# Masked and first units' values one unit later, value weights behind x, x stored block by block

## The chip, the cores and the metric

The kernel runs on the 8 cores of one Trainium2 chip. Every core does the whole transformer layer for one of the eight sequences and talks to no other core, so the program is the same everywhere. The metric is the device time in microseconds of the slowest core; lower is better.

## The reference

```python
x = _layernorm(x + attn(x))        # x: (8, 4096, 1024), one sequence per core
x = _layernorm(x + ffn(x))
# attn: qkv = x @ Wqkv.T + b; 16 heads of 64; causal softmax(q k.T / 8) v; @ Wproj.T + b
# ffn:  gelu(x @ w1 + b1) @ w2 + b2, hidden width 4096
```

The products run in bfloat16 with float32 sums in PSUM.

## The kernel before

**Stages.** A core first computes attention for 8 pairs of heads (p = 0 to 7), each over 8 blocks of 512 queries (g = 0 to 7), and then goes through 16 blocks of 256 tokens with the output projection, the first norm and the feed-forward layer. x lies transposed in the tile `xT` during attention: 128 partitions, and per partition 8 feature chunks (fc) of 4096 tokens each, so that token block g of chunk fc begins at column 4096 fc + 512 g. The input in DRAM (`xb`) is laid out by block.

**Units.** Attention is a list of 1088 units (p, g, j). A unit is one key tile j of 128 keys against the 512 queries of block g for both heads of pair p: scores (L593, TensorE, into one of two pairs of PSUM banks, by the unit's parity), exp (L610, ScalarE, into one of 7 buffers `pbuf`), for the tiles on the diagonal a mask (L621, VectorE), and the values (L665, TensorE: 8 matmuls of 65 columns for each 128 queries, into banks 6 and 7). A block has 4g + 3 units; the last three are on the diagonal (j = 4g, 4g + 1, 4g + 2; the second also carries tile 4g + 3). The first eight blocks of pairs 0 and 1 alternate, then the pairs follow one after another. After a block's last values VectorE divides by the row sums (`divide`, L688 and L690), which also frees banks 6 and 7 for the next block's first unit; some units later `turn_block` transposes the result (L704), copies it (L708) and stores it in DRAM.

**What sets the order.** The instruction order of each engine is written out by the loop at L944. Iteration i puts any waiting halves of values, scores of unit i + 1, exp of unit i, again halves of values, perhaps one `turn_block`, and then fill: `run_fill` takes steps from the queue `fill` by a credit that spreads them up to the unit that needs them. The fill steps are the projections of q and k (`qk_steps` L284, `qk_pairs` L452/L453), their row norms for the exp's bound (L312, L512), and the values' projection (`v_steps` L375, `v_pairs`). Each step has a `need` and a `free`, the first unit at which it may be put. `waiting` holds units whose values are not yet queued: the oldest is queued at iteration i once i minus its number reaches `hold`, which is 3 for a block's first unit (j = 0) and 2 otherwise. `run_halves` puts a unit's values in two halves of 64 key rows, the second only after something else was put between.

**Start.** `pool.dma` issues on GpSimd's queue, in this order: q and k weights of pair 0 (two pieces `wqk0_0`, `wqk0_4`), x of block 0 in four pieces of two chunks each, and the value weights of the first group in two pieces (`wv0_0`, `wv0_4`), interleaved as w, x, wv, x, w, x, wv, x; then the weights of pair 1, x of blocks 1 to 7, and more weights. Each piece is 256 KB as it lies on chip. SyncE's queue brings the mask (`tri`, behind x's first piece), biases and the identity. Meanwhile TensorE does 40 matmuls on constants (`warm`, L239). `first_block` then does, chunk by chunk, the q and k projection (`go`, L404: two matmuls of 512 columns) and the values' projection (`go_v`, L412: four matmuls of 256 columns) of block 0, then VectorE adds the bias (L423), TensorE does the scores of unit 0 and the two norm sums (L431), VectorE the maxima (L435) and the bound (L329, L338), and last the values' evacuation (L439). ScalarE's first instruction is the exp of unit 0, ahead of which the table is loaded.

**Other loads.** `wp` is loaded into `wpT` at the head of block (3, 1), behind pair 2's last values, because pair 2's q and k lie there; the first eight pieces of w2 are issued at the head of (7, 1), behind pair 6's last values and the w1 pieces. At the head of (7, 0) GpSimd adds the projection's bias to two blocks of x (`add_bias`, L774).

Of the kernel before, what the change touches and what calls it, by code (L numbers as in the profile page):

```python
# [10 lines left out]
AF = mybir.ActivationFunctionType  # L11
# [75 lines left out]
def build_nc():  # L87
# [115 lines left out]
    xTv = xT.rearrange("p (f g c) -> p f g c", f=8, g=NG)  # L203
    ld_bqk = sp.dma(slot("bqk"), bqk, bqk_d)
    first_x, ld_qk0, ld_v0 = [], [], []
    wqk0 = wqk[0].rearrange("p (i c) -> p i c", i=2)
    wqk0_d = wqk_d[0].rearrange("p (i c) -> p i c", i=2)
    for f in range(0, 8, 2):
        if f % 4 == 0:
            ld_qk0.append(pool.dma(slot(f"wqk0_{f}"), wqk0[:, :, 128 * f : 128 * f + 512],  # L210
                                   wqk0_d[:, :, 128 * f : 128 * f + 512]))
        first_x.append(pool.dma(
            slot(f"x0_{f}"), xTv[:, f : f + 2, 0, :],
            xb_d[0][:, QB * f : QB * f + 2 * QB].rearrange("p (f c) -> p f c", f=2)))
        if f % 4 == 0:
            ld_v0.append(pool.dma(slot(f"wv0_{f}"), wv[0][:, 256 * f : 256 * f + 1024],
                                  wv_d[0][:, 256 * f : 256 * f + 1024]))
    ld_qk[0], ld_v[0] = ld_qk0[1], ld_v0[1]
    ld_qk[1] = pool.dma(slot("wqk1"), wqk[1], wqk_d[1])
    for g in range(1, NG):  # L220
        ld_x[g] = pool.dma(slot(f"x{g}"), xTv[:, :, g, :],
                           xb_d[g].rearrange("p (f c) -> p f c", f=8))
# [13 lines left out]
    def warm():  # L236
        a = None
        for _ in range(40):
            r = t.matmul(bank(6), ones, sq[0], start=True, stop=True)  # L239
            a = a or r  # L240
        return a, r
    warm_done = pe.put(warm, t_warm, t_ones)
# [28 lines left out]
    def qk_steps(p, qi, g):  # L271

        st = {}
        w = wqk[QK_AT[p]]

        def step(fc):
            def go():
                if fc == 0:
                    st["b"] = gbank(True)
                b = st["b"]  # L280
                last = fc == 7
                gb_open[b] = not last
                tok = pe.put(
                    lambda: t.matmul(  # L284
                        bank(4 + b),
                        w[:, 1024 * qi + 128 * fc : 1024 * qi + 128 * fc + 128],
                        xT[:, S * fc + QB * g : S * fc + QB * g + QB],
                        start=fc == 0, stop=last),
                    *((gb_free[b], ld_qk[p], ld_x[g]) if fc == 0 else ()), mark=last)
                if last:  # L290
                    dst = (q2 if qi == 0 else k2)[p][:, QB * g : QB * g + QB]
                    ev = dve.put(
                        lambda: v.tensor_scalar(
                            dst, bank(4 + b), bqk[:, 8 * qi + p : 8 * qi + p + 1], None, ALU.add),
                        tok, ld_bqk, q2_done.get(QK_FROM.get(p)))
                    gb_free[b] = ev
                    t_qk[p, qi, g] = ev
                    wqk_done[p] = tok
            return go
        return [(1.0, step(fc)) for fc in range(8)]  # L300
# [58 lines left out]

    def v_steps(vp, a):  # L360
# [4 lines left out]
        def step(h):  # L365
            def go():
# [5 lines left out]
                for fc in (2 * h, 2 * h + 1):  # L372
# [4 lines left out]
                            xT[:, S * fc + 128 * a : S * fc + 128 * a + 128],  # L377
# [17 lines left out]
    def first_block():  # L395
# [4 lines left out]
        def go(fc):  # L400
            r = a = None
            for qi in range(2):
                o = 1024 * qi + 128 * fc
                r = t.matmul(bank(4 + qi), wqk[0][:, o : o + 128], xT[:, S * fc : S * fc + QB],  # L404
                             start=fc == 0, stop=fc == 7)
                a = a or r
            return a, r

        def go_v(fc):
            r = a = None  # L410
            for n in range(4):
                r = t.matmul(bank(6 + n // 2)[:, 256 * (n % 2) : 256 * (n % 2) + 256],  # L412
                             xT[:, S * fc + 128 * n : S * fc + 128 * n + 128],
                             wv[0][:, 256 * fc : 256 * fc + 256],
                             start=fc == 0 and n % 2 == 0, stop=fc == 7, skip_group_check=True)
                a = a or r
            return a, r
        for fc in range(8):
            tok = pe.put(lambda fc=fc: go(fc), first_x[fc // 2], ld_qk0[fc // 4], mark=fc == 7)
            tok_v = pe.put(lambda fc=fc: go_v(fc), ld_v0[fc // 4], mark=fc == 7)  # L420
# [15 lines left out]
        bound(0, 0)  # L436
        for a in range(4):
# [30 lines left out]
    def qk_pairs(p, g):  # L468
# [4 lines left out]
        def step(n):  # L473
            def go():
# [6 lines left out]
                xs = slice(S * fc + QB * g, S * fc + QB * g + QB)  # L481
# [41 lines left out]
    def v_pairs(vp, a):  # L523
# [4 lines left out]
        def step(n):  # L528
            def go():
# [4 lines left out]
                c0, c1 = (S * fc + 128 * (a + b0), S * fc + 128 * (a + b1))  # L534
# [370 lines left out]
    for p, g in blocks:  # L905
        if p > 1 or g > 3:
            need = start_of[p, g] if p < NPAIR - 1 else start_of[p, 0]
            later.append((need, qk_pairs(p, g) + norm_pair(p, g), start_of[p - 1, 0] + 3 if p > 2 else 0))
            if p % 2 == 0:
                vs = [x for a in range(4 * g, 4 * g + 4, 2) for x in v_pairs(p // 2, a)]  # L910
                later.append((need + 4 * g, vs, start_of[p - 2, 0] + 3 if p > 2 else 0))
# [31 lines left out]

    for i, (p, g, j) in enumerate(units):  # L944
        if j == 0:
            if (p, g) == (3, 1):
# [8 lines left out]
            if p == NPAIR - 1 and g == 1:  # L955
                load_w2(0, 8, q2_done[NPAIR - 2])
# [17 lines left out]
        hold = 3 if units[waiting[0]][2] == 0 and i + 1 < NU else 2  # L974
        while waiting and i - waiting[0] >= hold:
            queue_values(waiting.popleft())
            hold = 2
# [190 lines left out]
```

How the kernel before makes its waits and increments, by code:

```python
    def run(self):  # L54
        seen = {}
        for emit, after, inc in self.items:
            waits = {}
            for tok in after:
                if tok is None:
                    continue
                sem, val = tok
                if seen.get(sem, 0) >= val:
                    continue
                waits[sem] = max(waits.get(sem, 0), val)
            for sem, val in waits.items():
                seen[sem] = val
            todo = list(waits.items())
            held = todo.pop() if (todo and self.fuse) else None
            for sem, val in todo:
                self.eng.wait_ge(sem, val)
            done = emit()
            first, last = done if isinstance(done, tuple) else (done, done)
            if held is not None:
                first.wait_op(held[0], held[1], "sem-ge")
            if inc is not None:
                last.then_inc(inc[0], inc[1])
```

## Time and profile before

| what | us |
|---|---|
| median of 3 runs | 2211.36 |
| the three runs | 2211.36, 2312.66, 2210.08 |
| the profiled execution | 2209.44 |
| its span on the slowest core (core 1) | 2207.9 |
| spans of the 8 cores | 2200.8 to 2207.9 |
| granted TensorE clock, mean of core 1 | 0.986 |
| TensorE matmuls busy (PE) | 2059.6 |
| ScalarE busy (ACT) | 1328.7 |
| VectorE busy (DVE) | 743.2 |

The profile is of one execution on its slowest core, in microseconds from its first instruction. PE is TensorE's matmuls, PEld its weight loads, DVE VectorE, ACT ScalarE, POOL GpSimd, SPq SyncE's queue. A row of a group of instructions gives line, engine, operation, output<-input by tile (many tiles share the name `work`), shapes and count, busy time and the mean of one in ns, and then the engine's idle time before them with what ended it. A busy time of several matmuls run together ends with the last one's pipeline, so it is not the spacing times their number. The clock is 1.00 for 2.4 GHz and 0.50 for 1.2 GHz.

### The profile page before, as it was taken

The numbers are of one execution on the slowest core, as the hardware profiler recorded it, in microseconds if no ns is written. First come the engines' busy times: TensorE is split into PE (matmuls) and PEld (weight loads), VectorE is DVE, ScalarE is ACT, GpSimd is POOL, SyncE is SP. The second block draws the span as 40 slices with busy tenths as digits, with TensorE's granted clock in tenths as the row PEclk, the third lists the DMA queues.
The fourth block names the chain that finished last, engine by engine and source line by source line (L and its number), as shares of the span: only waits on it lengthen the run. The fifth ranks groups of instructions, "written<-read, shape, count | busy, mean of one in ns | idle before, by whom it ended". The sixth has DMA issues, their size and how long they took to land.

```text
span 2207.9 us, 65222 instructions; the slowest of 8 cores (2200.8 to 2207.9 us)
## 1 busy us (share of the span) xinstructions
PE 2059.6 (93%) x30380; PEld 1299.5 (59%) x30380; DVE 743.2 (34%) x1925; ACT 1328.7 (60%) x1602; POOL 219.2 (10%) x182
## 2 busy tenths in 40 slices
PE   7999998989999999997788999999999999999997
PEld 3455565555565556654445666666666666666665
DVE  3543334344343443435121322333223223332321
ACT  1799999999999999998995222222222222222222
POOL 2000000000000000001011221222111112221100
PEclk8999999999999999999899999999999999999999
DMA  9500100021000000002954201111110011111000
GB/s 144 81 12 8 36 8 12 19 34 35 8 13 19 8 24 8 12 10 66 169 88 89 51 27 48 49 49 49 48 48 20 30 48 48 48 48 49 20 20 20
DMA packets 53184, 89.73 MB, mean 41 GB/s; under 512 B 3248, under 2 KB 36656, under 8 KB 51888
## 3 DMA queue, kind: packets, MB, share of 16 engines
q0 software_dynamic: 17184, 33.56, 10.0%
q1 hardware_dynamic: 35728, 52.00, 7.1%
q8 instruction: 237, 3.88, 0.7%
q14 instruction: 35, 0.29, 0.0%
HBM read 93.94 MB, written 25.17 MB: 54 GB/s over the span
## 4 chain that ended last, share of the span: by engine, by line
PE 61%; ACT 29%; DVE 7%; DMA 1%; issue 1%; POOL 0%; POOLq 0%; SPq 0%; DVEq 0%; ACTq 0%
ACT work L610 29%; PE ps L1010 20%; PE ps L1028 19%; PE ps L815 5%; PE ps L452 5%; PE ps L665 4%; PE ps L593 4%; DVE qkv L493 2%; DVE work L621 1%; PE ps L284 1%; PE ps L512 1%; DVE work L690 1%; DMA xT<-xb 1%; DVE stat L517 1%; PE ps L858 1%
## 5 line engine op out<-in xcount | busy, mean ns | idle before, releaser
L610 ACT ACTIVATE work<-ps,cb 128x1024 bf16<-128x1024 f32 (+1 forms) x1088 | 1083.8, 1123 | 66.6 <-PE ps L593 61.6
L1018 ACT ACTIVATE work<-ps,b_s 128x256 bf16<-128x256 f32 x512 | 242.3, 473 | 764.1 <-PE ps L1010 764.1
L665 PEld LDWEIGHTS ps<-qkv,work 64*128 64x128 bf16 x16896 | 434.6, 95 | 292.7 <-PE ps L665 82.7
L665 PE MATMUL ps<-qkv,work 64*128 64x65 bf16 x16896 | 569.8, 193 | 17.9 <-DVE work L690 11.6
L1010 PE MATMUL ps<-work,xT 128*128 128x256 bf16 x4096 | 532.2, 273 | 0.4 <-issue 0.4
L1028 PE MATMUL ps<-qkv,work 128*128 128x512 bf16 x1984 | 509.0, 379 | 0.0
L1010 PEld LDWEIGHTS ps<-work,xT 128*128 128x128 bf16 x4096 | 401.3, 98 | 156.2 <-issue 0.5
L593 PE MATMUL ps<-qkv 64*128 64x512 bf16 x2016 | 366.4, 369 | 65.4 <-ACT work L610 57.8
L1028 PEld LDWEIGHTS ps<-qkv,work 128*128 128x128 bf16 x1984 | 192.9, 98 | 164.1 <-ACT work L1018 0.2
L452 PE MATMUL ps<-xT,work 64*128 64x512 bf16 x896 | 258.3, 377 | 2.9 <-DVE stat L517 1.8
L453 PE MATMUL ps<-xT,work 64*128 64x512 bf16 x896 | 258.4, 377 | 0.0
L593 PEld LDWEIGHTS ps<-qkv 64*128 64x128 bf16 x2016 | 94.5, 94 | 114.5 <-ACT work L610 93.4
L621 DVE TENSOR_TENSOR work<-work,tri_s 128x128 bf16<-128x128 bf16 x512 | 92.2, 238 | 199.5 <-ACT work L610 199.3
L815 PE MATMUL ps<-wpT,work 128*128 128x512 bf16 x512 | 146.3, 380 | 0.8 <-DMA work<-attn_s 0.6
L1054 DVE TENSOR_TENSOR work<-ps,work 128x512 f32<-128x512 f32 x64 | 39.8, 684 | 309.0 <-PE ps L1028 309.0
L452 PE MATMUL ps<-work,xT 64*128 64x256 bf16 x896 | 134.0, 269 | 3.4 <-DVE stat L517 1.8
L453 PE MATMUL ps<-work,xT 64*128 64x256 bf16 x896 | 134.0, 269 | 0.0
L493 DVE TENSOR_SCALAR qkv<-ps,bqk_s 128x512 bf16<-128x512 f32 x96 | 67.5, 745 | 156.5 <-PE ps L453 156.5
L774 POOL TENSOR_TENSOR work<-work,bvb 128x1024 f32<-128x1024 f32 x32 | 75.2, 2351 | 422.8 <-DMA work<-x 420.3
L788 POOL TENSOR_TENSOR lnst<-lnst,cexp 128x1 f32<-128x1 f32 x64 | 35.1, 548 | 629.5 <-DVE lnst L787 627.5
L790 DVE SCALAR_TENSOR_TENSOR lnst<-lnst 128x1 f32<-128x1 f32 x64 | 10.2, 160 | 234.2 <-POOL lnst L788 234.2
L546 DVE TENSOR_TENSOR qkv<-ps,bvb 128x256 bf16<-128x256 f32 x112 | 42.4, 421 | 136.0 <-PE ps L453 136.0
(74 smaller groups left out, 1262.2 us busy)
## 6 DMA issues: line engine op xcount, KB each, us to landing
work<-x SPq DMA_DIRECT2D x16, 1024.0 KB, 6.3
out<-work SPq DMA_DIRECT2D x15, 1024.0 KB, 4.1
attn_s<-work SPq DMA_DIRECT2D x64, 128.0 KB, 2.0
xT<-w POOLq DMA_DIRECT2D x8, 1024.0 KB, 14.6
work<-attn_s SPq DMA_DIRECT2D x16, 512.0 KB, 7.7
qkv<-w POOLq DMA_DIRECT2D x16, 512.0 KB, 8.3
xT<-xb POOLq DMA_DIRECT2D x7, 1024.0 KB, 45.4
work<-wqk POOLq DMA_DIRECT2D x7, 512.0 KB, 6.1
```

Of the source, the lines that this page charges most:

```text
L452: x = t.matmul(out0, lhs0, rhs0, start=start, stop=stop, skip_group_check=True)
L453: y = t.matmul(out1, lhs1, rhs1, start=start, stop=stop, skip_group_check=True)
L493: lambda qi=qi, dst=dst: v.tensor_scalar(dst, bank(4 + qi), bqk[:, 8 * qi + p : 8 * qi + p + 1], None, ALU.add),
L593: b = t.matmul(PS[:, o : o + 512 - q0], k2[p][64 * h : 64 * h + 64, 128 * jt : 128 * jt + 128], q2[p][64 * h : 64 * h + 64, QB * g + q0 : ...
L610: lambda: sc.activation(pb, ps, AF.Exp, bias=cb[:, 8 * p + g : 8 * p + g + 1], scale=0.125),
L621: b = v.tensor_tensor(q, q, tri_s, ALU.mult)
L665: r = t.matmul(bank(6 + h)[:, 65 * c : 65 * c + 65], pbuf[i % NP][rows, pc : pc + 128], w[rows, o : o + 65], start=first and j == 0 and c ...
L774: lambda c=c: gp.tensor_tensor(xbuf[n][:, 1024 * c : 1024 * c + 1024], xbuf[n][:, 1024 * c : 1024 * c + 1024], bpb, ALU.add),
L815: lambda: t.matmul(out_bank, atb[b % 2][:, 256 * k + 128 * c : 256 * k + 128 * c + 128], wpT[:, 1024 * k + 512 * oh : 1024 * k + 512 * oh ...
L1010: r = t.matmul(bank(4 + ui % 2)[:, 0:TB], w1[:, FF * f + 128 * hc : FF * f + 128 * hc + 128], x2T[b % 2][:, TB * f : TB * f + TB], start=f ...
L1018: lambda: sc.activation(hbuf[ui % 4], bank(4 + ui % 2)[:, 0:TB], AF.Gelu, bias=b1[:, hc : hc + 1]),
L1028: r = t.matmul(bank(2 * c + oh), hbuf[ui % 4][:, 128 * c : 128 * c + 128], w2[hc][:, 512 * oh : 512 * oh + 512], start=hc == 0, stop=hc == 31)
```

## The change

The change has five parts. (1) The value weights `wv0` come in one transfer behind the four pieces of x, and `go_v` is now put once, behind the two norm sums and ahead of the scores of unit 1, instead of chunk by chunk between the q and k projections. (2) `xT` is laid out by block: block g begins at column 4096 g, with its 8 chunks of 512 inside; a transfer's run in a partition becomes 2 KB (pieces) or 8 KB (blocks) where it was 1 KB. (3) `warm` is 26 matmuls ahead, and 3, 3, 3 and 4 more behind each pair of chunks. (4) ScalarE does a small exp at the start. (5) A unit's values are queued 4 units after it for j = 0, 3 for the diagonal's units, and 2 otherwise; `free` of later pairs' fill goes from + 3 to + 6, `wp` from (3, 1) to (3, 2), and w2 from (7, 1) to (7, 2).

```diff
@@ start: the transfers
-        first_x.append(pool.dma(
-            slot(f"x0_{f}"), xTv[:, f : f + 2, 0, :],
-            xb_d[0][:, QB * f : QB * f + 2 * QB].rearrange("p (f c) -> p f c", f=2)))
-        if f % 4 == 0:
-            ld_v0.append(pool.dma(slot(f"wv0_{f}"), wv[0][:, 256 * f : 256 * f + 1024],
-                                  wv_d[0][:, 256 * f : 256 * f + 1024]))
-    ld_qk[0], ld_v[0] = ld_qk0[1], ld_v0[1]
+        first_x.append(pool.dma(slot(f"x0_{f}"), xT[:, QB * f : QB * f + 2 * QB],
+                                xb_d[0][:, QB * f : QB * f + 2 * QB]))
+    ld_qk[0] = ld_qk0[1]
+    ld_v[0] = pool.dma(slot("wv0"), wv[0], wv_d[0])
     ld_qk[1] = pool.dma(slot("wqk1"), wqk[1], wqk_d[1])
     for g in range(1, NG):
-        ld_x[g] = pool.dma(slot(f"x{g}"), xTv[:, :, g, :],
-                           xb_d[g].rearrange("p (f c) -> p f c", f=8))
+        ld_x[g] = pool.dma(slot(f"x{g}"), xT[:, 8 * QB * g : 8 * QB * g + 8 * QB], xb_d[g])
@@ warm-up and table
-    def warm():
+    def warm(n):
         a = None
-        for _ in range(40):
+        for _ in range(n):
             r = t.matmul(bank(6), ones, sq[0], start=True, stop=True)
             a = a or r
         return a, r
-    warm_done = pe.put(warm, t_warm, t_ones)
+    pe.put(lambda: warm(26), t_warm, t_ones)
+    act.put(lambda: sc.activation(lnst[:, 0:1], cexp[:, 0:1], AF.Exp), t_cexp)
@@ qk_steps (and alike in v_steps, first_block, qk_pairs, v_pairs)
-                        xT[:, S * fc + QB * g : S * fc + QB * g + QB],
+                        xT[:, 8 * QB * g + QB * fc : 8 * QB * g + QB * fc + QB],
+    def x_col(a, fc):
+        return 8 * QB * (a // 4) + QB * fc + 128 * (a % 4)
@@ first_block
-        def go_v(fc):
+        def go_v():
             r = a = None
             for n in range(4):
-                r = t.matmul(bank(6 + n // 2)[:, 256 * (n % 2) : 256 * (n % 2) + 256],
-...
+                for fc in range(8):
+                    r = t.matmul(bank(6 + n // 2)[:, 256 * (n % 2) : 256 * (n % 2) + 256],
+                                 xT[:, x_col(n, fc) : x_col(n, fc) + 128],
+                                 wv[0][:, 256 * fc : 256 * fc + 256],
+                                 start=fc == 0 and n % 2 == 0, stop=fc == 7, skip_group_check=True)
+                    a = a or r
             return a, r
         for fc in range(8):
             tok = pe.put(lambda fc=fc: go(fc), first_x[fc // 2], ld_qk0[fc // 4], mark=fc == 7)
-            tok_v = pe.put(lambda fc=fc: go_v(fc), ld_v0[fc // 4], mark=fc == 7)
+            if fc % 2 == 1:
+                warm_done = pe.put(lambda: warm(3 if fc < 7 else 4), t_warm, t_ones)
...
         bound(0, 0)
+        tok_v = pe.put(go_v, ld_v[0])
@@ fill of later pairs
-            later.append((need, qk_pairs(p, g) + norm_pair(p, g), start_of[p - 1, 0] + 3 if p > 2 else 0))
+            later.append((need, qk_pairs(p, g) + norm_pair(p, g), start_of[p - 1, 0] + 6 if p > 2 else 0))
...
-                later.append((need + 4 * g, vs, start_of[p - 2, 0] + 3 if p > 2 else 0))
+                later.append((need + 4 * g, vs, start_of[p - 2, 0] + 6 if p > 2 else 0))
@@ main loop
+    def behind(p, g, j):
+        return 4 if j == 0 else 3 if j >= 4 * g else 2
...
-            if (p, g) == (3, 1):
+            if (p, g) == (3, 2):
...
-            if p == NPAIR - 1 and g == 1:
+            if p == NPAIR - 1 and g == 2:
                 load_w2(0, 8, q2_done[NPAIR - 2])
...
-        hold = 3 if units[waiting[0]][2] == 0 and i + 1 < NU else 2
-        while waiting and i - waiting[0] >= hold:
+        while waiting and (i + 1 == NU or i - waiting[0] >= behind(*units[waiting[0]])):
             queue_values(waiting.popleft())
-            hold = 2
```

## Rows read from the trace of the kernel before

**Rows 1.** the page: engines, then exp and values (busy us, mean ns | idle).

```profile
PE 2059.6 (93%) x30380; PEld 1299.5 (59%) x30380; DVE 743.2 (34%) x1925; ACT 1328.7 (60%) x1602; POOL 219.2 (10%) x182
...
L610 ACT ACTIVATE work<-ps,cb 128x1024 bf16<-128x1024 f32 (+1 forms) x1088 | 1083.8, 1123 | 66.6 <-PE ps L593 61.6
...
L665 PE MATMUL ps<-qkv,work 64*128 64x65 bf16 x16896 | 569.8, 193 | 17.9 <-DVE work L690 11.6
```

**Rows 2.** by stretch: length, busy us of PE, PEld, DVE, ACT, POOL; clock, DMA, GB/s.

```profile
30.00:119.00 89.00, 78.22 (x1112) 37.93 (x1108) 48.75 (x138) 56.22 (x54) 0.00 (x0) 0.97 0.65 98
119.00:1034.00 915.00, 838.24 (x19741) 520.70 (x19738) 367.32 (x1099) 891.30 (x897) 4.60 (x8) 1.00 0.08 19
1034.00:1060.00 26.00, 15.67 (x338) 10.01 (x336) 15.49 (x33) 18.82 (x21) 11.15 (x7) 0.74 0.61 123
1060.00:1182.00 122.00, 94.74 (x2216) 58.39 (x2216) 26.38 (x83) 118.76 (x121) 14.15 (x17) 0.93 0.60 101
1182.00:2207.90 1025.90, 1010.33 (x6894) 662.56 (x6886) 280.55 (x560) 243.59 (x513) 175.95 (x128) 0.99 0.14 44
```

**Rows 3.** the timeline's DMA issues: start us, length, engine, line, operation, transfer.

```profile
10.15 0.33 SPq L50 DMA_DIRECT2D tri_s<-tri  x1
...
25.58 0.33 SPq L50 DMA_DIRECT2D bvb<-bv  x1
```

**Rows 4.** the timeline of TensorE, VectorE, ScalarE, 3 to 32 us; idle before in brackets.

```profile
3.05 10.88 PE L239 MATMUL ps<-work,ones 128*128 128x512 bf16 x40 [3.05 <-DVE work L234]
...
16.80 0.60 PE L412 MATMUL ps<-work,xT 128*128 128x256 bf16 x4
...
18.88 0.59 PE L404 MATMUL ps<-xT,work 128*128 128x512 bf16 x2 [1.47 <-DMA xT<-xb]
...
22.73 1.03 PE L404 MATMUL ps<-xT,work 128*128 128x512 bf16 x2 [0.77 <-DMA xT<-xb]
...
25.26 1.06 PE L412 MATMUL ps<-work,xT 128*128 128x256 bf16 x4
...
25.59 1.41 DVE L423 TENSOR_SCALAR qkv<-ps,bqk_s 128x512 bf16<-128x512 f32 x2 [22.60 <-PE ps L404]
...
27.59 1.03 PE L431 MATMUL ps<-work,ones 128*128 128x512 bf16 x2
...
29.59 0.61 PE L593 MATMUL ps<-qkv 64*128 64x384 bf16 x4 [0.96 <-DVE stat L435]
...
30.00 1.28 ACT L610 ACT_TABLE_LOAD   x1 [30.00 <-DVE cb L338]
...
30.13 5.38 PE L284 MATMUL ps<-xT,work 128*128 128x512 bf16 x14
...
31.29 2.12 ACT L610 ACTIVATE work<-ps,cb 128x1024 bf16<-128x1024 f32 x2
```

**Rows 5.** busy times before and after the clock's first fall, columns as in the second group.

```profile
16.80:20.97 4.17, 2.12 (x14) 1.07 (x13) 0.00 (x0) 0.00 (x0) 0.00 (x0) 1.00 1.09 178
20.97:34.60 13.63, 11.16 (x36) 4.10 (x35) 6.17 (x16) 3.40 (x3) 0.00 (x0) 0.50 1.00 147
```

**Rows 6.** waits of ScalarE and TensorE, 119 to 1034 us; total, times, longest.

```profile
ACT work L610 <- PE ps L593: 23.6, 50, 2.1
...
PE ps L665 <- DVE work L690: 8.2, 21, 0.8
```

**Rows 7.** groups of instructions, 1034 to 1046 us.

```profile
L621 DVE TENSOR_TENSOR work<-work,tri_s 128x128 bf16<-128x128 bf16 x16 | 10.3, 719 | 3.3 <-ACT work L610 3.3
L774 POOL TENSOR_TENSOR work<-work,bvb 128x1024 f32<-128x1024 f32 x4 | 9.6, 2390 | 264.9 <-DMA work<-x 264.5
...
L665 PE MATMUL ps<-qkv,work 64*128 64x65 bf16 x82 | 3.1, 196 | 4.3 <-DVE work L621 4.3
```

**Rows 8.** the tile xT, 0 to 130 us: durations ns minimum/median/maximum, and DMA landing.

```profile
L284 PE MATMUL ps<-xT,work x112: 376/379/634, 30.1 to 115.3; 128*128 128x512 bf16 x112
...
L50 POOL DMA_DIRECT2D xT<-xb x11: 713/873/889, 2.5 to 12.8; - x11
...
DMA to landing us min/median/max: 7.6/34.4/63.8
```

More of the change, by code:

```diff
@@ L202, in build_nc @@
     ld_v = {}
-    xTv = xT.rearrange("p (f g c) -> p f g c", f=8, g=NG)
     ld_bqk = sp.dma(slot("bqk"), bqk, bqk_d)
-    first_x, ld_qk0, ld_v0 = [], [], []
+    first_x, ld_qk0 = [], []
     wqk0 = wqk[0].rearrange("p (i c) -> p i c", i=2)
@@ L376, in go @@
                             bank(4 + b)[:, 0:256],
-                            xT[:, S * fc + 128 * a : S * fc + 128 * a + 128],
+                            xT[:, x_col(a, fc) : x_col(a, fc) + 128],
                             w[:, 256 * fc : 256 * fc + 256],
@@ L403, in go @@
                 o = 1024 * qi + 128 * fc
-                r = t.matmul(bank(4 + qi), wqk[0][:, o : o + 128], xT[:, S * fc : S * fc + QB],
+                r = t.matmul(bank(4 + qi), wqk[0][:, o : o + 128], xT[:, QB * fc : QB * fc + QB],
                              start=fc == 0, stop=fc == 7)
@@ L407, in go @@
             return a, r
-        def go_v(fc):
+        def go_v():
             r = a = None
             for n in range(4):
-                r = t.matmul(bank(6 + n // 2)[:, 256 * (n % 2) : 256 * (n % 2) + 256],
[L413 to L416, printed above, removed]
+                for fc in range(8):
[4 more added lines that the diff above has]
+                    a = a or r
             return a, r
@@ L480, in go @@
                 o1 = 1024 * qi1 + 128 * fc
-                xs = slice(S * fc + QB * g, S * fc + QB * g + QB)
+                xs = slice(8 * QB * g + QB * fc, 8 * QB * g + QB * fc + QB)
                 tok = two_tiles(
@@ L533, in go @@
                 b0, b1 = (1, 0) if turned else (0, 1)
-                c0, c1 = (S * fc + 128 * (a + b0), S * fc + 128 * (a + b1))
+                c0, c1 = x_col(a + b0, fc), x_col(a + b1, fc)
                 ws = slice(256 * fc, 256 * fc + 256)
```

## The prediction

> **What bounds the kernel now.** I read the page's busy times first, then busy times by stretch, the timeline of the start, the waits, and the groups around the one large stall. TensorE is busy 2059.6 us and ScalarE 1328.7, which says little by itself [rows 1]. The stretches say more [rows 2]. From 1182 us on TensorE is busy 1010.3 of 1025.9 us: the feed-forward stage is TensorE's, and no part of the change touches it. From 119 to 1034 us ScalarE is busy 891.3 of 915 us: there the exps set the pace, and the most that any reordering can give is the 23.7 us that ScalarE stands idle. From 30 to 119 us ScalarE is busy only 56.2 of 89 us while TensorE is busy 78.2: the projections of the first blocks must be caught up with, so a microsecond won ahead of this stretch is passed on to its end. Before 30 us nothing is computed that ScalarE could use: it waits until 30.00 and loads its table until 31.29 [rows 4]. Over the whole span the exp's engine was idle 66.6 us ahead of its exps, 61.6 of it for scores [rows 1]. That is 3.0% of the span and the ceiling of the attention parts.
>
> **The start.** x's first piece had landed by 10.15 us [rows 3], its last at 22.73 [rows 4]. Between them lie six pieces of 256 KB, 12.6 us, 2.1 us each; the last two took 22.73 - 18.88 = 3.85 us, 1.9 each. Two of the eight, the value weights, go behind x, so the last piece lands 3.9 to 4.2 us earlier, at about 18.7 us. GpSimd issues in the same queue, one transfer fewer; its issue of a piece takes 0.7 to 0.9 us [rows 8] and ends long before the landing, so it stays covered.
>
> At 22.73 us the clock had already fallen to 0.50 (it fell at 20.97 and came back at 34.60 [rows 5]), and eight value matmuls stood between and behind the last four of q and k, so VectorE's bias began only at 25.59, 2.86 us behind the landing [rows 4]. Two 512-column matmuls take 0.59 us at the full clock and 1.03 at half [rows 4], where one alone takes 0.38 and 0.63 [rows 8]: a spacing of 0.21 and about 0.42. The four that are left cost 0.9 or 1.7 us. The bias then begins at 19.6 us at the full clock; at half it begins at 20.4, or at 21.3 if the two matmul pairs and three warm-ups ahead are late as well.
>
> From the bias to the bound were 30.00 - 25.59 = 4.4 us, with the two norm sums at half clock (1.03 us; 0.59 at full). The table's 1.28 us [rows 4] now lies at the start, where ScalarE has nothing else. The first exp moves from 31.29 to 23.6 (full) or 25.7 us (half).
>
> That is not yet the gain, since the values' projection no longer sits in the shadow of the transfers: 32 matmuls of 256 columns now stand in TensorE's queue ahead of the scores of unit 1. Four take 0.60 us at full and 1.06 at half clock [rows 4], a spacing of 0.11 and 0.21: 3.5 or 6.9 us for all. They begin behind the norm sums, 3.0 us (2.6 at full) behind the bias, and not before their weights, which end the same eight pieces as before and so land near 22.8 us. At the full clock: 22.8 + 3.5 = 26.3, scores of unit 1 by 26.9, then the first fill, 14 matmuls that took 5.38 us from 30.13 [rows 4] and take 13 x 0.21 + 0.38 = 3.1 at full. They end at 30.0 where they ended at 35.5: 5.5 us won. At half: values from 24.3; before, the clock returned at 34.60 after 5 us of steady work from 29.59 [rows 4, 5]; if it does the like, at 29.3, the values end near 30.2 and the fill at 33.9: 1.6 us won. Which of the two? Before, 2.12 busy us of 4.17 were followed by the fall [rows 5]. Now, from the end of 26 warm-ups (14 fewer of 0.21 us, so about 10.9 us) to 18.7 us there are three rounds of four matmuls and three warm-ups, 7 x 0.21 = 1.5 us each, 4.5 us of 7.8, 58% against 51%. That is too near to promise the full clock; the fall may come somewhat later. I take **3.0 us**, with 1.6 and 5.5 as ends.
>
> The layout of x changes no matmul: each still reads 512 contiguous columns of a partition. For the transfers the rows leave room for a gain: pair 1's weights, 512 KB in 4 KB runs, landed 2.85 us behind x's last piece (25.58 - 22.73 [rows 3, 4]), 180 KB per us; the seven blocks of x behind them, 7168 KB in 1 KB runs, landed 63.8 us after an issue at 12.8 [rows 8], so at 76.6, 141 KB per us. At the better rate x's four pieces would land 1.5 us earlier. But the pieces of the start moved at 256 / 1.9 = 135 KB per us whatever their runs, so I take 0, and keep -1.5 as an end. The Trainium skill, DMA: Bandwidth & Descriptors, section Specifications, has line rate from 512 bytes on, by which 1 KB runs already had it and this part gives nothing; the 141 against 180 speaks for a difference, and measurement would decide. No wait of the start is on blocks 1 to 7, so their faster landing is worth nothing.
>
> On the table the Trainium skill, ScalarE: Activation LUTs, section What ACT_TABLE_LOAD costs, has 1.28 us and about 1.38 of drain for a switch. The trace agrees with the first (1.28) and shows no second: the exp begins at 31.29, where the load ends [rows 4]. By the page the start would give 1.4 us more.
>
> **The stall at 1034 us.** GpSimd's four adds (9.6 us) make 16 masks take 10.3 us, 0.65 each, and TensorE waits 4.3 us for masks in values that stand ahead of scores [rows 7]. From 1034 to 1060 us ScalarE is idle 7.2 us, and the clock is at 0.74 [rows 2]. The adds and the masks stay. One unit more lies between a mask and its values, so one more exp can run first, at most an exp's 1.0 us (891.3 / 897 [rows 2]) and the clock's share of it. I take **1.5 us**, between 0 and 3.
>
> **The other turns.** From 119 to 1034 us TensorE's waits on this side are for the divide (8.2 us, 21 times) and not for masks, which the view does not list at all [rows 6]. The change does not help the divide: the last unit's values move by one (2 to 3) and the next first unit's by one (3 to 4), so the divide has the same two units. What moves is where the matmuls lie. When the first unit's values are queued, two other units' come at once instead of one. I take **0.5 us** of gain; the ends are a third of the 23.6 us of waits [rows 6], -8, and +8, the divide's waits doubled.
>
> **Moved loads.** `wp` waits for pair 2's last values, now a unit (1.0 us) later, and is read some 500 us later; on GpSimd's queue nothing is put between. The w2 pieces stand behind the w1 pieces in the same queue, so their place in the program costs nothing. If w2's cover were gone the feed-forward stage would show it as a wait of at most the moved seven units, 7 us. `free` + 6 binds only where fill is that far ahead; where it binds, 3 units of about 1 us do without fill and catch up by at most 3 steps each, five times: 0 to 5 us, taken as 0.
>
> The sum: 2209.4 (the profiled execution; its span is 2207.9) - 3.0 - 1.5 - 0.5 = 2204.4, rounded to **2204 us**. The profiled execution lies 2.0 us under the median of the runs, 2211.36, so against that the gain is 7 us, 0.3%.
>
> **Rivals.** (a) Start's gain lost: the clock falls early, stays at half through the values and does not return with them, so that the second scores are as late as before and only the other terms stay: 2207 to 2210. For it speaks the 51% row; against it that the values and fill are now one steady run. (b) Slower: the values bunch. At some 60 turns two held units come behind a first one, and TensorE has little room to catch up: it is busy 838 of 915 us, 0.09 us free per exp [rows 2]. A unit's values are 569.8 / 1088 = 0.52 us [rows 1]. If all of that comes ahead of scores and isn't absorbed, 60 x 0.52 = 31 us are lost: 2204 + 31 = 2235. It decides as soon as the extra unit exceeds what the one pair of scores computed ahead can cover, about an exp less its scores, 0.6 us; 0.52 is under it, and the present hold of 3 already bunches one unit and costs at most the 23.6 us of all waits. So rather a third of it, 2215, if it comes. (c) The turns gain for real: half of the ScalarE waits of 23.6 go, and the start keeps its 5.5: 2204 - 12 - 2.5 = 2190. For it: 50 waits of half a us are of a size with one unit's shift. (d) Part of the change doesn't do what it says: ScalarE's table could be loaded at the first exp anyway, 1.3 us less gain; 2206, inside the forecast.
>
> **How the numbers follow.** The forecast, 2199 to 2208, has 0.5; (a) 0.17; (b) 0.16; (c) 0.14; anything outside 0.03. The range 2190 to 2217 holds the forecast, (a), most of (c) and the lower half of (b). Faster by over 2% would need 44 us, two thirds of all idle time ahead of exps: 0.01. Slower by over 2%, more than (b) in full: 0.02. Within 2%, about what a measurement of this kernel can tell from no change: 0.97.
>
> **What would show it.** The bias on q and k near 20 us instead of 25.59; a table load before 5 us and the first exp near 24 to 26; the clock's first fall later than 20.97 or missing; `L284`'s first fourteen ending between 30 and 34 instead of 35.5; ScalarE's waits from 119 to 1034 near 23 us; its idle time from 1034 to 1060 nearer 6 than 7.2. Waits above 32 us there would show (b), under 14 (c). The stage from 1182 on must keep its 1026 us; if it doesn't, the prediction is wrong in a part I costed at nothing.

## The result and the profile after

The change made the kernel slower: the ratio to the kernel before is 1.0063, 95% interval 1.0044 to 1.0082, about 14 us on 2210. The medians of 13 runs each are 2223.72 and 2210.89 us; the profiled execution took 2220.25 us, its span was 2218.7 (2207.9 before). The predicted 2204 was wrong in sign, and the median lies above the whole predicted range, 2190 to 2217. Some executions of either kernel are disturbed, up to 2490 us, and are left out of all ratios.

The start, from the timeline of the changed kernel (start us, length, engine, line, operation, tiles, count, idle before), answers to [rows 3, 4]. Its lines are numbered anew: L280 was L284, L404 stays, L413 is the values' projection, L613 the exp (L610), L668 the values (L665), L693 the divide (L690), L707 the transposes (L704), L624 the mask (L621). L515 is the pairs' norm sums (L512), L501 the VectorE step ahead of them (L498).

```profile
1.05 1.28 ACT L238 ACT_TABLE_LOAD   x1 [1.05 <-PEq L88]
...
16.04 1.02 PE L404 MATMUL ps<-xT,work 128*128 128x512 bf16 x4 [1.03 <-DMA xT<-xb]
...
17.41 0.32 SPq L50 DMA_DIRECT2D idb_s<-idb  x1
17.77 1.03 PE L404 MATMUL ps<-xT,work 128*128 128x512 bf16 x4
...
18.91 1.41 DVE L425 TENSOR_SCALAR qkv<-ps,bqk_s 128x512 bf16<-128x512 f32 x2 [15.93 <-PE ps L404]
...
21.27 3.66 PE L413 MATMUL ps<-work,xT 128*128 128x256 bf16 x32
...
22.90 1.11 ACT L613 ACTIVATE work<-ps,cb 128x1024 bf16<-128x1024 f32 x1 [20.18 <-DVE cb L334]
...
25.18 3.19 PE L280 MATMUL ps<-xT,work 128*128 128x512 bf16 x14
...
41.42 0.69 ACT L613 ACTIVATE work<-ps,cb 128x512 bf16<-128x512 f32 x1 [7.02 <-PE ps L596]
```

x's last piece has landed by 17.41 us, where the identity behind it is issued, instead of at 22.73. The bias begins at 18.91 instead of 25.59. The first fill's fourteen matmuls end at 28.37 instead of 35.51 [rows 4], 7.1 us ahead. That sets core 0 of the changed kernel against core 1 of the kernel before, whose start was the latest of its eight. Core by core the same matmuls end 1.9 to 6.3 us earlier, 4.3 on the mean (28.4 against 32.7), so the start is ahead by less than the 7.1 suggests. By stretches the changed kernel reads (columns as in [rows 2]):

```profile
0.00:30.00 30.00, 24.63 (x117) 11.22 (x117) 8.71 (x23) 4.25 (x5) 9.77 (x21) 1.00 0.95 141
30.00:119.00 89.00, 76.61 (x1205) 38.54 (x1207) 46.42 (x137) 57.31 (x57) 0.00 (x0) 1.00 0.54 94
119.00:1034.00 915.00, 828.56 (x19414) 514.26 (x19414) 363.69 (x1083) 877.29 (x882) 4.63 (x8) 0.99 0.08 17
1034.00:1192.00 158.00, 117.72 (x2737) 73.78 (x2733) 45.16 (x118) 146.43 (x149) 25.34 (x24) 0.89 0.61 109
1192.00:2218.70 1026.70, 1011.20 (x6920) 663.22 (x6919) 281.37 (x565) 245.08 (x515) 176.12 (x128) 0.99 0.14 43
```

The feed-forward stage has its time, 1026.7 us for 1025.9. From 119 to 1034 us ScalarE is idle 37.7 us where it was 23.7 (means of the eight cores: 35.8 and 22.5), and did 882 exps where it did 897. So the place is the turns. The prediction's sign for its rival (b), ScalarE's waits there above 32 us, has come (36.1), but it can't tell bunched values from another cause at the same turns. The waits of that stretch in the changed kernel (engine and line, what it waited for: total us, times, longest) answer to [rows 6]:

```profile
ACT work L613 <- PE ps L596: 36.1, 64, 1.7
PE ps L596 <- ACT work L613: 40.7, 118, 0.6
PE ps L515 <- DVE work L501: 15.5, 25, 1.3
PE ps L707 <- DVE work L693: 14.6, 12, 1.9
PE ps L515 <- DVE work L711: 2.3, 5, 0.8
PE ps L707 <- DVE qkv L496: 2.0, 7, 0.5
PE ps L668 <- DVE work L693: 1.9, 5, 0.4
```

The fourth row is new. TensorE waited 14.6 us in 12 waits for the divide ahead of the transposes; before, no such row was there. The values' own wait for the divide fell from 8.2 to 1.9 us. One turn in the changed kernel's timeline shows the damage:

```profile
632.61 0.69 DVE L693 TENSOR_TENSOR work<-ps,rden 128x512 bf16<-128x512 f32 x1
633.36 0.61 PE L707 MATMUL ps<-idb_s,work 128*128 128x128 bf16 x4 [1.81 <-DVE work L693]
633.90 0.40 PE L668 MATMUL ps<-qkv,work 64*128 64x65 bf16 x8
634.07 0.42 DVE L711 COPY work<-ps 128x512 bf16<-128x512 bf16 x1 [0.77 <-PE ps L707]
634.11 0.62 PE L596 MATMUL ps<-qkv 64*128 64x512 bf16 x2
...
634.77 1.11 ACT L613 ACTIVATE work<-ps,cb 128x1024 bf16<-128x1024 f32 x1 [1.66 <-PE ps L596]
635.10 1.03 PE L515 MATMUL ps<-work,ones 128*128 128x512 bf16 x2
```

TensorE stands 1.81 us at the transposes, the scores behind them come late, ScalarE is idle 1.66 us, and then two 512-column matmuls take 1.03 us: the granted clock fell to 0.50 (1.2 GHz) near 633.2 us, at the end of the wait.

### The profile page after: what moved, and what is told of

Read it like the earlier page. It is cut to its first block, busy times and chain, and to the rows that moved or that the text cites. A ratio compares the mean times of both kernels' runs of the same rounds, so it can differ in the third digit from the quotient of the medians.

```text
span 2218.7 us, 65228 instructions; the slowest of 8 cores (2214.8 to 2218.7 us)
## 1 busy us (share of the span) xinstructions
PE 2058.7 (93%) x30382; PEld 1301.0 (59%) x30382; DVE 745.4 (34%) x1925; ACT 1330.4 (60%) x1603; POOL 215.9 (10%) x181
## 4 chain that ended last, share of the span: by engine, by line
PE 62%; ACT 28%; DVE 8%; issue 1%; DMA 1%; POOL 0%; POOLq 0%; ACTq 0%; DVEq 0%
ACT work L613 28%; PE ps L1016 20%; PE ps L1034 19%; PE ps L455 5%; PE ps L818 5%; PE ps L668 5%; PE ps L596 4%; DVE qkv L496 2%; PE ps L515 1%; DVE work L624 1%; DVE work L693 1%; PE ps L280 1%; PE ps L707 1%; DVE work L501 1%; PE ps L1043 1%
## 5 line engine op out<-in xcount | busy, mean ns | idle before, releaser
L613 ACT ACTIVATE work<-ps,cb 128x1024 bf16<-128x1024 f32 (+1 forms) x1088 | 1084.7, 1114 | 105.5 <-PE ps L596 80.7
L668 PEld LDWEIGHTS ps<-qkv,work 64*128 64x128 bf16 x16896 | 430.7, 96 | 267.7 <-PE ps L668 81.5
L668 PE MATMUL ps<-qkv,work 64*128 64x65 bf16 x16896 | 558.3, 193 | 6.4 <-DVE work L624 4.2
L624 DVE TENSOR_TENSOR work<-work,tri_s 128x128 bf16<-128x128 bf16 x512 | 92.7, 239 | 192.7 <-ACT work L613 191.8
```

The source lines that it names most:

```text
L613: lambda: sc.activation(pb, ps, AF.Exp, bias=cb[:, 8 * p + g : 8 * p + g + 1], scale=0.125),
L624: b = v.tensor_tensor(q, q, tri_s, ALU.mult)
L668: r = t.matmul(bank(6 + h)[:, 65 * c : 65 * c + 65], pbuf[i % NP][rows, pc : pc + 128], w[rows, o : o + 65], start=first and j == 0 and c ...
```

## The experiments

The theory after the result, D: the last unit's values come one unit later, but `turn_block` is still put 5 units after the block's last unit, so the transposes now stand one unit behind the divide in TensorE's queue instead of two, with scores behind them. Rivals: B, the held units' values bunch behind the first one; F, the fill held back to + 6; L, the new layout; S, the start's gain does not last.

**The start alone.**

```diff
-        while waiting and (i + 1 == NU or i - waiting[0] >= behind(*units[waiting[0]])):
+        hold = 3 if units[waiting[0]][2] == 0 and i + 1 < NU else 2
+        while waiting and i - waiting[0] >= hold:
             queue_values(waiting.popleft())
+            hold = 2
# free + 3, wp at (3, 1), w2 at (7, 1), as before
```

> The changed kernel with the order of values, free and the places of the loads as before, so parts 1 to 4 alone. In the profile of the changed kernel the fourteen matmuls of the first fill ended 7.1 us earlier (28.37 against 35.51 us), and at 54 us the exps were still 7.0 us ahead. Theory T (the start gives its 7 us, the order of the values takes it back and more): 2203 to 2205 us against 2211 before. Rival S (the start's gain is lost again somewhere in the projections' stretch whatever the order): 2208 to 2212. Rival L (the new layout of x slows the matmuls or transfers later): 2215 and more.

Ratio 0.998, interval 0.9962 to 0.9997; median 2204.03. L falls. The start gains about 4.4 us by the ratio and 7.5 by the medians; the ratio's interval reaches from 8 us to under 1, so the time alone does not rule S out. The traces do better. On the mean of the eight cores the exp that the rows above have at 41.42 us stands at 41.9 us, where it was 46.4 before; GpSimd's first add at the head of pair 7 stands at 1027.0, where it was 1031.2; ScalarE's table load at the end of attention stands at 1179.7, where it was 1182.6. So 4.5 us are won at the start, 4.1 last through the projections' stretch to the head of pair 7, against S, and 2.9 are left behind attention. T's direction holds; its 7 us were too much.

**The order alone**, the kernel before with part 5.

```diff
-        hold = 3 if units[waiting[0]][2] == 0 and i + 1 < NU else 2
-        while waiting and i - waiting[0] >= hold:
+        while waiting and (i + 1 == NU or i - waiting[0] >= behind(*units[waiting[0]])):
# free + 6, wp at (3, 2), w2 at (7, 2)
```

> The kernel before with part 5 alone: values of masked units 3 and of first units 4 behind, free + 6, wp and w2 a block later. Theory T: 12.8 us measured loss of the whole plus 7 us of the start, so 2228 to 2232 us. Rival L (layout): about 2211. If the two parts do not add (the order costs only because the start is ahead), 2215 to 2222.

Ratio 1.0093, interval 1.0078 to 1.0108, some 20 us; the profiled execution took 2229.49. The transposes' wait is there again, with the start as it was:

```profile
PE ps L704 <- DVE work L690: 14.5, 11, 1.9
```

The time is the one that T asked for, 2228 to 2232. The parts add within their intervals: -0.2% and +0.93% against +0.63%.

**The transposes one unit later.**

```diff
-        while turns and i - turns[0][0] >= 5 and not (gb_open[0] and gb_open[1]) and i >= ready[0]:
+        while turns and i - turns[0][0] >= 6 and not (gb_open[0] and gb_open[1]) and i >= ready[0]:
```

> The changed kernel with the transposes of a finished block put no earlier than 6 units after its last unit, where it was 5. The last values now end a unit later, so at 5 the transposes stand directly behind the divide in TensorE's queue, ahead of scores. Theory D (the loss at the turns is TensorE's wait of the transposes for the divide, 14.6 us in 12 waits from 119 to 1034 us, 0 before): the wait goes to under 3 us, time 2206 to 2212. Rival B (the values of three units come at once behind the first unit): the transposes' wait may go but the time stays within 3 us of 2222. Rival F (free + 6 and the burst of fill behind it): no change either, 2220 to 2224.

Ratio 0.9994, interval 0.998 to 1.0009. One number takes back 0.69% of the kernel's time, most of the 0.83% that lie between the changed kernel and the start alone, and of the transposes' 14.6 us of waiting 2.0 are left. ScalarE's waits stay above those of the start alone, 28.0 us against 20.3:

```profile
ACT work L613 <- PE ps L596: 28.0, 58, 1.3
...
PE ps L668 <- DVE work L693: 5.2, 14, 0.5
...
PE ps L707 <- DVE work L693: 2.0, 2, 1.8
```

**The transposes one unit sooner, values where they were.** The converse, on the start alone: only the distance is shortened.

```diff
-        while turns and i - turns[0][0] >= 5 and not (gb_open[0] and gb_open[1]) and i >= ready[0]:
+        while turns and i - turns[0][0] >= 4 and not (gb_open[0] and gb_open[1]) and i >= ready[0]:
```

> The start alone, values where they were before, with the transposes put from 4 units after a block's last unit, where it was 5. Only their distance to the divide is as short as in the changed kernel; nothing is bunched and no values are later. Theory D (that distance alone makes the loss): TensorE waits 12 to 18 us in about a dozen waits for the divide ahead of the transposes from 119 to 1034 us, and the time goes from 2204 to 2214 to 2220 us. Rival B (the later values' bunching makes it): 2203 to 2207.

Ratio 1.0032, interval 1.0004 to 1.0059; median 2216.35. No unit's values are later here and no more of them are queued at once, yet the kernel is 0.5% slower than the start alone, with the same kind of wait:

```profile
PE ps L707 <- DVE work L693: 12.1, 9, 2.8
```

So the distance by itself makes a loss, 0.5% here, of the 0.83% that the whole order costs on top of the start. D holds in both directions.

**Only first units later.**

```diff
-        return 4 if j == 0 else 3 if j >= 4 * g else 2
+        return 4 if j == 0 else 2
```

> The changed kernel with only first units one later (4), masked units at 2 as before. The last unit's values and the divide are then as early as before, but at the first unit's turn three units' values are queued at once, as in the changed kernel. Theory D: the transposes do not wait, and the time is that of the start's part, 2203 to 2208. Rival B (bunching): about as slow as the changed kernel, 2218 to 2224.

Ratio 0.9995, interval 0.9985 to 1.0004; median 2210.38. The transposes wait for the divide once, 0.8 us, the values once, 0.4 us. It queues three units at once, as the changed kernel does, and lies 13 (medians) to 15 us (ratios) below it; but it lies above the start alone, by 0.15%, with intervals that overlap, and its median is 2 us over D's range. A small price of bunching three is not ruled out.

**Only masked units later.**

```diff
-        return 4 if j == 0 else 3 if j >= 4 * g else 2
+        return 3 if j == 0 or j >= 4 * g else 2
```

> The changed kernel with masked units 3 behind and first units at 3 as before, transposes still at 5. The last unit's values and so the divide are a unit later, the next first unit's values are not. Theory D: the transposes wait as in the changed kernel (12 to 16 us), and the first unit's values now wait for the divide too, so it is as slow or slower, 2220 to 2232 us. Rival B (bunching of three units is what costs): without a bunch it is back at 2204 to 2210.

Ratio 1.0182, interval 1.0168 to 1.0197, and a median of 2250.39, slower than was expected even of D. The mechanism is D's, the place another: the next block's first values now stand one unit behind the divide and take the wait ahead of the transposes. The rows are of core 4, whose span is 2245.0 us:

```profile
PE ps L668 <- DVE work L693: 44.8, 47, 2.7
PE ps L596 <- ACT work L613: 29.1, 87, 0.5
```

44.8 us in 47 waits at the turns, against 8.2 in 21 [rows 6]. B asked for a return to the time before, since no three units are queued at once; the kernel is 40 us slower than that.

**First units five behind.** The changed kernel with transposes at 6, `free` + 3, and

```diff
-        return 4 if j == 0 else 3 if j >= 4 * g else 2
+        return 5 if j == 0 else 3 if j >= 4 * g else 2
```

> The changed kernel with transposes at 6 and free + 3, masked units 3 behind and first units 5 instead of 4, so that three units lie between the last values of a block and the first of the next, and four units' values are then queued at once. Theory D (only the distance to the divide counts): the waits of values for the divide, 5.2 us with 4, go to under 1 us and the time is 2203 to 2206. Rival B (bunching has a price that grows with the units queued at once): 2210 to 2222.

Ratio 1.0041, interval 1.0028 to 1.0054. Here the theory's number missed and B's came (median 2219.04): the values' wait for the divide went to 1.0 us as expected, yet the kernel is 0.5% slower than with 4. From 119 to 1034 us ScalarE was busy 882.3 us (886.3 in the last kernel of this section, with 4). Its waits show what the theory had left out:

```profile
ACT work L613 <- PE ps L596: 24.3, 50, 1.3
...
ACT work L613 <- PE ps L668: 5.2, 6, 2.2
...
PE ps L707 <- DVE work L693: 4.9, 3, 1.8
```

The second row is new: exps wait for values. An exp writes one of seven buffers and must wait until the values of seven units before have read it; with four units' values queued late, that becomes a limit. So a price of the kind that B foretold is there with four units. Its mechanism is in part the buffers: 5.2 us of waits in this stretch, 22.3 us in 18 waits over the first 1200 us. How much of the 10 us of loss they make is not shown, since the waits for scores fell meanwhile (24.3 here, 28.0 with 4 and the transposes at 6).

**Fill free at + 3 in the changed kernel.**

```diff
-            later.append((need, qk_pairs(p, g) + norm_pair(p, g), start_of[p - 1, 0] + 6 if p > 2 else 0))
+            later.append((need, qk_pairs(p, g) + norm_pair(p, g), start_of[p - 1, 0] + 3 if p > 2 else 0))
# and alike for the values' fill
```

> The changed kernel with the fill's free units back at + 3; values and start as changed. Theory D (transposes wait for the divide): nothing moves, 2219 to 2225 us, the transposes' wait from 119 to 1034 us stays at 13 to 16 us. Rival F (fill held back by 6 and then put in a burst): 2208 to 2214.

Ratio 1.0058, interval 1.0044 to 1.0071; the transposes' wait is 14.9 us in 12. F falls: that edit costs nothing that can be measured, as predicted.

**The start alone without warm-ups between the pieces.**

```diff
-            if fc % 2 == 1:
-                warm_done = pe.put(lambda: warm(3 if fc < 7 else 4), t_warm, t_ones)
```

> The start alone (order of values as before) without the 3, 3, 3 and 4 warm-up matmuls between the pieces of x. Theory W (they hold the clock at 2.4 GHz): the granted clock falls before 20 us and the fourteen matmuls of the first fill end 2 to 5 us later than 28.4 us; 2206 to 2209 against 2204. Rival: two of eight pieces fewer to wait for and a steady run of values are enough, the clock stays, no difference (within 1 us of 2204).

Ratio 0.9997, interval 0.9978 to 1.0016; median 2208.09. In its profile the clock fell at 21.8 us for 3.4 us, in the middle of the values' projection:

```profile
15.83 1.02 PE L404 MATMUL ps<-xT,work 128*128 128x512 bf16 x4 [2.70 <-DMA xT<-xb]
...
21.17 5.33 PE L413 MATMUL ps<-work,xT 128*128 128x256 bf16 x32
...
26.76 3.19 PE L280 MATMUL ps<-xT,work 128*128 128x512 bf16 x14
```

The 32 matmuls took 5.33 us instead of 3.66, and the fill begins at 26.76 instead of 25.18 in the changed kernel, 1.6 us later. The mean granted clock from 14 to 30 us is below 1.00 on seven of this kernel's eight cores (0.79 to 0.89), against one of eight in the start alone (0.89) and none in the changed kernel. On the mean of the eight cores the first fill ends at 29.6 us against 28.6 in the start alone. So W holds in its mechanism, at 1 us and not at 2 to 5, and the fall came later than was expected; the ratio's distance to the start alone, 0.17%, has overlapping intervals and can't show so little.

**The start alone with x stored as before**, `xT` and its transfers by chunk.

```diff
-        first_x.append(pool.dma(slot(f"x0_{f}"), xT[:, QB * f : QB * f + 2 * QB],
-                                xb_d[0][:, QB * f : QB * f + 2 * QB]))
+        first_x.append(pool.dma(
+            slot(f"x0_{f}"), xTv[:, f : f + 2, 0, :],
+            xb_d[0][:, QB * f : QB * f + 2 * QB].rearrange("p (f c) -> p f c", f=2)))
# and alike for blocks 1 to 7 and all reads of xT
```

> The start alone with x stored as before, chunk by chunk in runs of 1 KB. Theory (the prediction's 0): x's last piece lands within 0.7 us of where it does with the new layout, and the time is 2203 to 2205 as with it. Rival (the 141 against 180 KB per us of the trace before are the runs' length): the last piece lands 1.5 us later, 2205 to 2206; the blocks of x behind land up to 10 us later, which nothing waits for.

Ratio 0.9998, interval 0.9988 to 1.0008; median 2209.7. Its time is that of the kernel before, so without the layout the start gives nothing that can be measured; the interval overlaps that of the start alone, and the traces must decide. Its timeline (L283 is the fill, L599 the scores):

```profile
17.89 0.32 SPq L50 DMA_DIRECT2D idb_s<-idb  x1
...
27.23 3.19 PE L283 MATMUL ps<-xT,work 128*128 128x512 bf16 x13 [1.60 <-DMA work<-wqk]
...
36.34 5.64 PE L283 MATMUL ps<-xT,work 128*128 128x512 bf16 x14 [2.68 <-DMA xT<-xb]
...
48.39 0.69 ACT L616 ACTIVATE work<-ps,cb 128x512 bf16<-128x512 f32 x1 [11.95 <-PE ps L599]
```

x's last piece lands where it does with the new layout (17.6 us in this and 17.5 in the changed kernel, means of eight cores), so the rival's 1.5 us are not there. But on this core pair 1's weights and block 1 behind it are late: 1.60 and 2.68 us of waiting, and behind the wait the clock is low (5.64 us for 14 matmuls). The exp that came at 41.42 us in the changed kernel comes at 48.39; on the mean of eight cores it stands at 46.0, against 46.4 before the change and 41.9 in the start alone, so the old layout loses nearly all that the start had won by then. On all eight cores of this kernel TensorE waits for block 1, 1.3 to 3.8 us; with the new layout 0 to 0.7. Only core 6 waits for the weights. Reckoned as in the prediction, the last block lands at 77.1 us (64.8 behind an issue at 12.3) against 72.6 in the changed kernel (63.1 behind 9.5). GpSimd also issues sooner with the new layout, a median of 0.57 us for a transfer of x and not 0.88. How the lateness splits between the transfers' rate and their issue was not taken apart.

**GpSimd's adds moved**, on the start alone.

```diff
                 load_x(1)
-                add_bias(0)
-                add_bias(1)
                 load_w1()
...
                 wqk_done[NPAIR - 1], wv_done[3], ld_w1[f - 2] if f > 1 else None))
+            if f in (5, 6):
+                add_bias(f - 5)
```

> The start alone with GpSimd's four bias adds behind the w1 pieces 5 and 6 of the same queue, where no mask is due, instead of at the head of block (7, 0). Theory G (the stall at 1034 us is the masks slowed by GpSimd's adds): the 16 masks fall from 0.65 to about 0.24 us each, ScalarE's idle time from 1034 to 1060 goes from 7 to 2 us, 2198 to 2201 against 2204. Rival (the w1 and x transfers and the emptier fill of pair 7 make the stall): no difference, or slower by up to 10 us if the w1 and w2 pieces behind the adds come late.

Ratio 0.9949, interval 0.9935 to 0.9963; median 2198.61, the fastest kernel of the study, as theory G asked, 0.3% below the start alone, whose interval it just touches. Its groups from 1034 to 1060 us (busy us, mean ns | idle before):

```profile
L613 ACT ACTIVATE work<-ps,cb 128x1024 bf16<-128x1024 f32 (+1 forms) x24 | 23.7, 1080 | 2.8 <-PE ps L596 2.8
...
L624 DVE TENSOR_TENSOR work<-work,tri_s 128x128 bf16<-128x128 bf16 x16 | 2.6, 221 | 5.7 <-ACT work L613 5.7
```

ScalarE is idle 2.8 us and not 7.2 there (7.0 in the start alone). The masks' mean hides how they were slowed. Their durations from 1034 to 1060 us (ns, minimum/median/maximum) in the kernel before and in this one:

```profile
L621 DVE TENSOR_TENSOR work<-work,tri_s x24: 210/214/2364, 1035.4 to 1053.9; 128x128 bf16<-128x128 bf16 x24
...
L624 DVE TENSOR_TENSOR work<-work,tri_s x16: 217/219/226, 1037.9 to 1052.6; 128x128 bf16<-128x128 bf16 x16
```

A mask takes 0.21 to 0.22 us in both. In the kernel before four masks, one to each of GpSimd's four adds (2.34 to 2.41 us), took 1.88 to 2.36 us and ended about where the add ended; the others were as fast as ever. So 0.65 us was an average of two kinds and described no mask. The stall is smaller here but not gone: the adds now lie between 1060 and 1072 us, and there two of eight masks are held again, so that six masks take 5.09 us where six take 0.94 elsewhere.

**All that the change wanted, with its two stalls cut down**: the changed kernel with transposes at 6, `free` + 3 and the adds moved.

```diff
-        while turns and i - turns[0][0] >= 5 and not (gb_open[0] and gb_open[1]) and i >= ready[0]:
+        while turns and i - turns[0][0] >= 6 and not (gb_open[0] and gb_open[1]) and i >= ready[0]:
# free + 3; add_bias(f - 5) behind the w1 pieces 5 and 6
```

> The changed kernel with transposes at 6, free + 3 and GpSimd's adds behind the w1 pieces 5 and 6: all that the change wanted, without its two stalls. Theory D and G: 6 us under the kernel with transposes at 6 (2207), so 2200 to 2203, and still 2 to 4 us over the start alone with the adds moved (2198.6), because the later values bring nothing. Rival (later values do bring something once the transposes wait no more): below 2198.

Ratio 0.9968, interval 0.9956 to 0.9981; median 2203.63. It lies 0.19% over the same kernel with the values where they were, with intervals that overlap a little (0.9956 to 0.9963). The rival's gain, below 2198, is not there: the later values bring nothing even where the transposes wait only 2.0 us for the divide and the values 5.2.

## Why the prediction was wrong

**The turns, where it failed.** The step was "The change does not help the divide: ... so the divide has the same two units", and from it a gain of 0.5 us with 8 of loss as the end. It counted the distance from the divide to one of its two readers, the next block's first values. The other reader, the transposes, was put 5 units after the block's last unit by a rule that the change left alone; when the last values moved by one, that distance shrank from two units to one. In place of at most 8 us of loss, the changed kernel's transposes waited 14.6 us in 12 new waits, and ScalarE's waits for scores in that stretch grew from 23.6 to 36.1 us. Both runs on the distance show it: one unit more gives back 0.69%, one unit less costs 0.5% with nothing else of the order changed. The divide's wait at the first reader did not stay the same either: it went from 8.2 to 1.9 us, in part because the transposes now stood ahead of it (5.2 us with them one unit later). The rival that ended on the slow side, bunching, had the right sign and, for most of the loss, the wrong mechanism: three units at once with an early divide cost 0.15% over the start alone, within the intervals. A price shows with four, 0.5%, in part through the exps' buffers. What is left of the later order with the transposes at 6, about 0.14% over the start alone, lies within the intervals, and its cause stays open.

**The start's size.** The mechanism was right and the term somewhat too small: 3.0 us taken, 4.3 in the traces at the first fill on the mean of the cores (7.1 between the two cores that the pages show), about 4.4 in the time by the ratio. The clock stayed at 1.00 in both stretches before 119 us of the profiled execution: of the prediction's two cases the better one came. The prediction read its start from the slowest core alone, which was also the latest. x's last piece came 4.9 us earlier on the mean (22.5 to 17.5; 5.3 between the cores shown), more than the 3.9 to 4.2 reckoned, and the run with the old layout puts nearly all of it to the order of the transfers, not to the layout.

**The layout was costed at nothing, wrongly.** "No wait of the start is on blocks 1 to 7, so their faster landing is worth nothing" was nearly true of the kernel before (none on the core shown, 0.3 to 0.9 us for block 1 on four others), but only of it: its late start was the cover. With the start earlier, the cover was gone, and the layout is what keeps the gain. The rule of the Trainium skill, DMA: Bandwidth & Descriptors, Specifications, that line rate begins at 512 bytes, would have 1 KB runs as good as 8 KB ones. The measurement speaks against taking the layout for free by that rule: with 1 KB runs the second fill waits for block 1 on all cores, 1.3 to 3.8 us; with 8 KB runs 0 to 0.7. The transfers' rate was not measured apart from their issue.

**The table** was right at 1.28 us: its load stands at 1.05 us in the profile after, and the first exp follows the bound at once, at 22.90 us. The 1.38 us of drain that the Trainium skill, ScalarE: Activation LUTs, What ACT_TABLE_LOAD costs, adds to a switch is not seen: before the change the exp began where the load ended [rows 4].

**The stall at 1034 us** gave none of its 1.5 us. In the changed kernel ScalarE's waits around it (from 1034 to 1070 us) are 7.9 us, where they were 7.1 over the same stretch before. TensorE's wait for masks is hardly shorter (4.0 us for 4.3), and the transposes' wait for the divide, 4.3 us, is new. The unit more between a mask and its values hardly helped. A likely reason, not tested: "0.65 each" in the prediction read a mean as the time of each mask, and a mask that is held 2.4 us outlasts the 1.0 us that one exp gives. The waits in the changed kernel:

```profile
ACT work L613 <- PE ps L596: 7.9, 6, 2.6
...
PE ps L707 <- DVE work L693: 4.3, 2, 2.8
```

**The moved loads and `free` + 6** were costed at nothing and cost nothing that shows: with `free` back the ratio is 1.0058 against 1.0063, and the stage from 1192 us on has its length. For `wp` and w2 only this length speaks; no run moved them alone.

## What to carry to other kernels

When an instruction is moved in an order written by hand, list every reader of its result and the rule that places each, not only the one the move is meant for; a reader placed by a fixed distance from something else silently loses slack, and in an in-order queue everything behind it pays. A transfer "that nothing waits for" is covered only as long as what covers it stays late: a faster start needs the next transfers costed again. Delaying work to shorten a wait is worth nothing where the view of waits does not list that wait. And a start that is read from one core should be set against the other cores too: which core is slowest, and by how much, changes from profile to profile.

## What the hardware showed that was not expected

A wait of TensorE can cost more than its length. In the changed kernel's profile the granted clock fell to 0.50 eight times between 119 and 1034 us, for 3.4 us each. Five of the falls came at the end of, or within about 2 us behind, a wait of 1.45 to 1.91 us of the transposes for the divide (near 125, 500, 514, 633 and 855 us), three behind a wait of 1.29 to 1.35 us of the norm sums for VectorE (near 278, 343 and 486 us). The kernel before had one fall in that stretch, of 6.8 us, and the start alone one of 3.4. Not every wait is followed by a fall (12 waits for the divide, five falls), and the kernel with the transposes at 6 still had six.

With three or four constant matmuls between the pieces of x the clock stayed at 2.4 GHz from 14 to 30 us on all eight cores of the changed kernel's profile and on seven of the start alone's; without them it fell there on seven of eight.

GpSimd's float32 adds on SBUF hold single bfloat16 masks of VectorE for up to the length of an add: four masks took 1.88 to 2.36 us beside adds of 2.34 to 2.41 us, and the others their 0.21 us.
